# Four graph layers on one core: stores of the first block on ScalarE's queue, and the last layer's aggregation with the adjacency tiles stationary

## The chip, the cores and the metric

The kernel runs on one core of a Trainium2 chip. The metric is the time of one execution on the device in microseconds (us). The core has five engines that run side by side and wait for one another by semaphores: TensorE (PE, matmuls), VectorE (DVE), ScalarE (ACT), GpSimd (POOL) and SyncE (SP, which here only issues transfers). Transfers (DMAs) are carried out by 16 DMA engines; an engine that issues one goes on at once, but an engine takes its instructions strictly in order, so one that waits ahead of an issue holds up everything behind it.

## The reference

The input is x (3327 nodes x 256 features, fp32) and adj (3327 x 3327, int32, about 1% ones, symmetric, with ones on the diagonal). Each of four layers adds a graph layer to x:

```
h = relu(layernorm(x));  x = x + layer(h, adj)
layer 0: 8-head attention (GAT): softmax over neighbours of leaky(el_i + er_j)
layer 1: attention by cosine similarity, masked by adj
layer 2: 8-head attention whose hard maximum is kept, masked by adj
layer 3: deg = sum_j mask_ij
         agg = (mask @ h) / max(deg, 1)
         out = relu([h @ W_self + b_self, agg @ W_nb + b_nb] @ W_comb + b_comb)
```

## The kernel before

Nodes are cut into NT = 26 tiles of P = 128 (NP = 3328), features into KC = 2 blocks of 128. k.X holds x in SBUF. Where fp16 isn't precise enough a number is kept as a high and a low fp16 half, and a product takes three matmuls for each feature block (`hi_lo_products`: high x high, high x low, low x high; six in all).

**startup** (lines 286 to 689) reads adj, transposes it with TensorE and stores it as fp8 in k.adjT, and between these projects h for layer 0. Its order is written out by hand in `startup_order`, and each engine walks the same list: `adj a` (transposes of one tile of 128 rows, in two halves of 13 blocks, L426; VectorE evacuates half 0, L661, ScalarE half 1, L537), `turn g` (normalise and transpose four tiles), `project t`, `left g` (the left attention terms of 512 nodes, to elT), `scale`, and 16 `factor` items (two exponentials x 8 heads). For a factor VectorE or GpSimd multiplies (F, ring of NF = 3), ScalarE copies to fp16 (L566, into X1, ring of NX = 3), VectorE subtracts for the low half (L656, semaphore s_xl), and the result is stored to xv_dram. SP walks the list too: at `adj i` it loads tile i + 2 into one of two slots once tile i has been transposed (L356, semaphore s_atr), at `left` it stores elT to el_dram (L375) once it is evacuated, at `factor` it stores X1 to xv_dram (L379):

```
elif kind == "factor":
    f, h = FACTORS[i]
    sp.wait_ge(s_xl, i + 1)
    sp.dma_start(xv_dram[f, h], X1[:, i % NX].rearrange("p t d -> p (t d)")).then_inc(s_out[i % NX], 16)
```

The tail of the list is: scale, adj 15, factors 0 and 1, adj 16, factor 2, adj 17, factors 3 and 4, adj 18, and so on to factor 14, adj 25, factor 15. Before `scale` goes on, all left terms must have landed (s_elo). The next stage, gat_sums, begins when all stores have landed.

**The last layer** (layer3) has two blocks. `normalise` computes statistics, h (H, fp32), its transpose hT as high and low halves (ScalarE L201, VectorE L169), and then `h_nat`, here Hn: h in natural layout as high halves (ScalarE L216) and low halves (VectorE L174), three pieces each. `mean_weights` runs inside it by hooks: it multiplies W_self and W_nb with their halves of W_comb (m, high L1766 and low L1722), makes the bias (L1751, L1725), and turns the inverse degrees round and stores them to ideg_dram. `mean_aggregate` is the second block. A chunk is CT = 2 tiles (256 nodes), NC = 13 of them. For each chunk `sums` makes the transposed aggregate: for each feature block 26 x 2 matmuls with Hn stationary and 256 columns of adjacency moving (104 in all, L1830). VectorE multiplies by the inverse degree (L1874), ScalarE takes the high half (L1860), VectorE the low half (L1877), and `linear` adds, for each tile, 6 matmuls of hT with m's own half (L1840) and 6 of the aggregate with the neighbour half (L1843). `linear` of a chunk comes behind the next chunk's `sums`. VectorE adds the bias (L1882), applies relu and adds to X (L1886). SP loads adjacency chunks from adjT_dram into two slots (L1794) and stores finished chunks.

Of the kernel before, what the change touches and what calls it, by code (L numbers as in the profile page):

```python
# [23 lines left out]
U8 = mybir.dt.uint8  # L24
# [63 lines left out]
def normalise(k, tag, hT, weights, h_nat=None, also=None):  # L88
# [8 lines left out]
    pieces = ((0, 9), (9, 18), (18, NT))  # L97
    COUNTED = 8
    with ExitStack() as c:
# [23 lines left out]
        def _(dve):  # L123
# [54 lines left out]
        def _(act):  # L178
# [34 lines left out]
            if h_nat is not None:  # L213
# [77 lines left out]
def startup(k, x_dram, adj_dram, w_lin, attn_w, el_dram, xv_dram, HC):  # L291
# [12 lines left out]
    NF, NX = 3, 3  # L304
# [9 lines left out]
    with ExitStack() as c:  # L314
# [33 lines left out]
        def _(sp):  # L348
# [19 lines left out]
            for kind, i in order:  # L368
                if kind == "adj" and i + 2 < NT:
                    load(i + 2)  # L370
                elif kind == "left":
                    c0, cn = CHUNKS[i]
                    at = items.index((kind, i))
                    sp.wait_ge(s_free[at % 2], at // 2 + 1)
                    sp.dma_start(el_dram[:, c0:c0 + cn], elT[:, i % 2, 0:cn]).then_inc(s_elo[i % 2], 16)  # L375
                elif kind == "factor":
                    f, h = FACTORS[i]
                    sp.wait_ge(s_xl, i + 1)
                    sp.dma_start(xv_dram[f, h], X1[:, i % NX].rearrange("p t d -> p (t d)")).then_inc(s_out[i % NX], 16)  # L379
# [111 lines left out]
        def _(act):  # L491
# [41 lines left out]

            for kind, i in order:
# [13 lines left out]
                elif kind == "turn":  # L548
                    relu(i + 1)
                    high(i)  # L550
                elif kind in ("project", "left"):
                    evacuate(kind, i)
                elif kind == "scale":
                    act.wait_ge(s_fac, 1)
# [5 lines left out]
                else:  # L560
# [5 lines left out]
                    nc.scalar.activation(X1[:, i % NX, :, 0:G1], F[:, i % NF], ACT.Copy).then_inc(s_xh, 1)  # L566

# [385 lines left out]


def over_chunks(eng, chunk):

    with eng.Fori(0, NC // 2) as i:
        chunk(2 * i, 0, False)
        chunk(2 * i + 1, 1, False)
    chunk(NC - 1, 0, True)  # L960
# [717 lines left out]
def mean_weights(k, c, ap, m, bias, ideg_dram):  # L1678
# [3 lines left out]
    s_in, s_tr, s_cp, s_bb, s_mm, s_hi, s_deg, s_rT, s_out, s_b = (  # L1682
        k.sem(f"s_w3_{n}") for n in ("in", "tr", "cp", "bb", "mm", "hi", "deg", "rT", "out", "b"))
# [7 lines left out]
    dT = k.sb(c, "w3_degT", [NT, P], F32)  # L1691
    pt = k.ps(c, "w3_pt", [P, 2, CH])
    pm = k.ps(c, "w3_pm", [P, 2, CH])
    pd, pb = pm[:, 1, :], pt[:, 0, :]
# [3 lines left out]
    def on_sync(sp):  # L1698
# [28 lines left out]
    def tensor_first(pe):  # L1727
        pe.wait_ge(s_deg, 2)
        nc.tensor.transpose(pd[0:NT, 0:P], dg[:, 1, :], k.ident[:]).then_inc(s_tr, 1)
# [7 lines left out]
        for s in range(2):  # L1737
            pe.wait_ge(s_cp, s + 1)
            if s == 1:
                pe.wait_ge(s_rT, 1)  # L1740
# [13 lines left out]
    def scalar_first(act):  # L1754
        act.wait_ge(s_tr, 1)
        nc.scalar.activation(dT[:], pd[0:NT, 0:P], ACT.Copy).then_inc(s_rT, 1)

    def scalar_mid(act):
        for s in range(2):
            act.wait_ge(s_tr, s + 2)  # L1760
            nc.scalar.activation(wt[:, s].rearrange("p k n -> p (k n)"), pt[:, s, :], ACT.Copy).then_inc(s_cp, 1)

    def scalar_last(act):
        for s in range(2):
# [4 lines left out]
            "scalar_first": scalar_first, "scalar_mid": scalar_mid, "scalar_last": scalar_last,  # L1769
# [3 lines left out]
def mean_aggregate(k, hT, Hn, m, bias, ideg_dram, adjT_dram, out_dram):  # L1773

    nc = k.nc
    s_agg, s_T, s_hi, s_lo, s_mm, s_t, s_x, s_ideg, s_st = (
        k.sem(f"s_m3_{n}") for n in ("agg", "T", "hi", "lo", "mm", "t", "x", "ideg", "st"))
    s_in = [k.sem(f"s_m3_in{i}") for i in range(2)]
    prods = hi_lo_products(KC)
    with ExitStack() as c:  # L1780
        ad = k.sb(c, "m3_ad", [P, 2, CT, NT, P], FP8)
        idr = k.sb(c, "m3_ideg", [P, NP], F32)
        T = k.sb(c, "m3_T", [P, 2, KC, CW], F32)
        aT = k.sb(c, "m3_aT", [P, 2, 2, KC, CW], F16)
        R = k.sb(c, "m3_R", [P, 2, CT, D], F32)
        pa = k.ps(c, "m3_pa", [P, 2, KC, CH])
        po = k.ps(c, "m3_po", [P, 2, CT, D])
# [3 lines left out]
        def _(sp):  # L1791
            def load(c, q):
                sp.wait_ge(s_agg, c + 1)
                sp.dma_start(ad[:, q].rearrange("p t j i -> p t (j i)").bitcast(U8),  # L1794
                             adjT_dram[bass.ds(c * CT, CT)].rearrange("t p n -> p t n").bitcast(U8)).then_inc(s_in[q], 16)

            def store(c):
                sp.wait_ge(s_x, c + 1)
                sp.dma_start(out_dram[bass.ds(c * CW, CW), :].rearrange("(t p) d -> p t d", p=P),
# [148 lines left out]
```

## Time and profile before

| | us |
|---|---|
| median of three runs | 2383.29 (2383.27 to 2383.88) |
| the profiled execution | 2383.7 |
| its span | 2381.7 |
| PE busy | 2105.3 (88%) |
| DVE busy | 1960.3 (82%) |
| ACT busy | 1779.1 (75%) |
| POOL busy | 732.4 (31%) |
| `startup` | 0 to about 188 |
| last layer | about 2145 to 2381.7 |

The span runs from the first to the last instruction or transfer that the profiler saw. Busy shares are averages over stages with different limits; the rows below are from the two stages that the change touches. Matmuls are pipelined: a matmul's duration in a row is longer than the distance at which they follow each other.

### The profile page before, as it was taken

What the parts mean: (1) busy time and instruction counts of PE and PEld (TensorE: products, weight loads), DVE (VectorE), ACT (ScalarE), POOL (GpSimd) and SP (SyncE); (2) the same over time, 40 slices, a digit from 0 to 9 for tenths busy, and PEclk for the clock granted to TensorE, in tenths of its full rate; (3) what the DMA queues carried; (4) which work ended last, traced back from release to release, by engine and by line L of the source; (5) the groups of instructions that cost most, each with busy time, mean ns of one, the idle gap of its engine ahead of it and who ended that gap; (6) DMA issues with size and microseconds to landing.
All of it is one profiled execution on the core that took longest, in us unless ns stands there. A gap on an engine that the chain in (4) does not pass through costs nothing. (4 is left out here: it accounts for less than half of the span.)

```text
span 2381.7 us, 62641 instructions
## 1 busy us (share of the span) xinstructions
PE 2105.3 (88%) x25316; PEld 1713.9 (72%) x25316; DVE 1960.3 (82%) x4332; ACT 1779.1 (75%) x2232; POOL 732.4 (31%) x698
## 2 busy tenths in 40 slices
PE   4747999999967999999979699999999999885999
PEld 3547999999954888888865366666666666554888
DVE  5575999999985888888878699999999999985122
ACT  4546999999975877777755499999999999994000
POOL 0020000000000000000003588888888888870000
PEclk9858999999988999999989799999999999996999
DMA  9787211212101111011006411111111111102222
GB/s 319 261 325 302 88 66 62 92 58 91 59 6 47 47 43 43 22 43 43 22 14 143 153 53 52 63 66 66 66 66 66 66 66 65 37 2 78 71 78 66
DMA packets 78475, 201.09 MB, mean 84 GB/s; under 512 B 26897, under 2 KB 44491, under 8 KB 74745
## 3 DMA queue, kind: packets, MB, share of 16 engines
q1 hardware_dynamic: 77432, 197.27, 24.5%
q8 instruction: 191, 3.13, 0.5%
q14 instruction: 84, 0.69, 0.1%
q10 hardware_dynamic: 768, 0.00, 0.0%
HBM read 161.87 MB, written 26.86 MB: 79 GB/s over the span
## 5 line engine op out<-in xcount | busy, mean ns | idle before, releaser
L1638 DVE CUSTOM_DVE_ANT_0 h_S<-h_ps,h_off 128x832 f32<-128x832 f32 x832 | 800.4, 1020 | 14.0 <-POOL h_off L1477 11.0
L1535 PE MATMUL h_ps<-KS,h_QS 98*128 98x416 f16 x1664 | 442.1, 348 | 79.8 <-DVE h_mx L1638 45.3
L1595 ACT ACTIVATE h_H<-h_S,h_nmx 128x2048 fp8e4<-128x2048 f32 x208 | 416.8, 2004 | 81.0 <-DVE h_nmx L1644 81.0
L834 ACT ACTIVATE b_CA<-b_el,HC 128x1152 fp8e4<-128x1152 f32 (+1 forms) x384 | 435.5, 1218 | 3.0 <-DMA b_el<-el_dram 3.0
L931 PE MATMUL b_pb<-b_x,b_B 128*128 128x132 f16 x5408 | 414.2, 221 | 3.9 <-DVE b_B L896 3.4
L931 PEld LDWEIGHTS b_pb<-b_x,b_B 128*128 128x128 fp8e4 x5408 | 340.3, 96 | 6.6 <-DVE b_B L896 6.2
L1483 POOL TENSOR_SCALAR h_gap<-h_S,h_nmx 128x1280 f32<-128x1280 f32 x208 | 277.8, 1336 | 89.2 <-DVE h_nmx L1644 79.6
L912 PE MATMUL b_pz<-b_x,adjT 128*128 128x134 f16 x2704 | 257.1, 222 | 15.9 <-DMA b_x<-xv_dram 15.9
L1488 POOL TENSOR_SCALAR h_H<-h_gap 128x1280 uint8<-128x1280 f32 x208 | 260.8, 1254 | 17.2
L1566 PEld LDWEIGHTS h_po<-Vhl,h_HT 128*128 128x128 fp8e4 x5408 | 214.6, 98 | 65.1 <-ACT h_HT L1602 0.7
L1245 PE MATMUL c_pd<-c_mv,WnT 128*128 128x256 f16 x2028 | 250.8, 275 | 11.0 <-DMA c_ad<-adjT_dram 11.0
L1535 PEld LDWEIGHTS h_ps<-KS,h_QS 98*128 98x128 f16 x1664 | 95.9, 97 | 198.3 <-DVE h_mx L1638 120.4
L1566 PE MATMUL h_po<-Vhl,h_HT 128*128 128x64 f16 x5408 | 225.7, 193 | 0.6 <-ACT h_HT L1604 0.6
L1245 PEld LDWEIGHTS c_pd<-c_mv,WnT 128*128 128x128 f16 x2028 | 199.8, 99 | 36.0 <-DMA c_ad<-adjT_dram 11.3
L1602 ACT ACTIVATE h_HT<-h_pT 128x1024 uint16<-128x1024 uint16 x208 | 209.6, 1008 | 0.2 <-PE h_pT L1543 0.2
L912 PEld LDWEIGHTS b_pz<-b_x,adjT 128*128 128x128 fp8e4 x2704 | 183.6, 97 | 16.1 <-DMA b_x<-xv_dram 16.1
L849 DVE TENSOR_SCALAR b_CD<-b_el,HC 128x1152 uint8<-128x1152 f32 (+1 forms) x240 | 187.5, 781 | 7.4 <-DMA b_el<-el_dram 7.4
L1155 ACT ACTIVATE c_E<-c_T,c_shift 128x512 f32<-128x512 f32 x169 | 122.3, 724 | 94.1 <-DVE c_T L1182 91.7
L1261 PE MATMUL c_pa<-WHhi,c_EH 128*128 128x257 f16 x676 | 185.4, 274 | 0.0
L1263 PE MATMUL c_pa<-WHhi,c_EL 128*128 128x257 f16 x676 | 184.7, 273 | 0.0
L1262 PE MATMUL c_pa<-WHlo,c_EH 128*128 128x256 f16 x676 | 184.1, 272 | 0.0
L1121 POOL MEMSET c_shift<- 128x1 f32 x1 | 0.1, 99 | 593.6 <-POOLq L971 593.6
(208 smaller groups left out, 3496.7 us busy)
## 6 DMA issues: line engine op xcount, KB each, us to landing
h_rows<-in_adj_dram SPq DMA_DIRECT2D x25, 1663.5 KB, 7.3
b_x<-xv_dram SPq DMA_DIRECT2D x48, 435.5 KB, 5.3
s_rows<-in_adj_dram SPq DMA_DIRECT2D x25, 832.0 KB, 6.7
s_rows<-in_adj_dram SPq DMA_DIRECT2D x25, 831.5 KB, 7.9
adjT_dram<-adjT SPq DMA_DIRECT2D x1, 10816.0 KB, 38.0
c_ad<-adjT_dram SPq DMA_DIRECT2D x13, 832.0 KB, 6.1
m_ad<-adjT_dram SPq DMA_DIRECT2D x13, 832.0 KB, 4.5
b_el<-el_dram SPq DMA_DIRECT2D x16, 576.0 KB, 3.7
```

What stands on the lines that cost most here:

```text
L834: nc.scalar.activation(dst[:, 0:cols], elr[:, n % 2, 0:cols], ACT.Sigmoid, bias=HC[:, h, 1, jt:jt + 1], scale=STEP, saturate=False).then_i ...
L849: nc.vector.tensor_scalar(dst[:, 0:gn * P].bitcast(U8), elr[:, n % 2, 0:gn * P], HC[:, h, 0, jt:jt + 1], float(FP8_ONE), ALU.is_gt, ALU.mu ...
L912: last = nc.tensor.matmul(pz[:, z % 2, r * WZ:(r + 1) * WZ].rearrange("p (h d) -> p h d", h=2), k.adjT[:, g0 + 3 * b + r, jt, :], xb[:, m ...
L931: last = nc.tensor.matmul(pb[:, p, b, r * W:(r + 1) * W].rearrange("p (f d) -> p f d", f=2), B[:, u % RING_B, t * P:(t + 1) * P], xb[:, m ...
L1245: last = nc.tensor.matmul(pd[:, n % RD, j * CW:(j + 1) * CW], WnT[:, a, kc, jt * P:(jt + 1) * P], mv[:, c % 2, b, kc, :], start=(i == 0), ...
L1483: nc.gpsimd.tensor_scalar(gap[:], S[:, g % 2, CA:NP], nmx[:, g % 2:g % 2 + 1], -SHARPER, ALU.add, ALU.mult).then_inc(s_gap, 1)
L1488: nc.gpsimd.tensor_scalar(H[:, g % 2, CA:NP].bitcast(U8), gap[:], float(FP8_ONE), 0.0, ALU.min, ALU.max).then_inc(s_hB, 1)
L1535: last = nc.tensor.matmul(ps[:, ch % 2, b, 0:SB], QS[:, i % 2, h, :], KS[:, h, c0:c0 + SB], start=True, stop=True)
L1566: last = nc.tensor.matmul(po[:, i % 2, h * 2 * HD:(h + 1) * 2 * HD], wt[:, b, :, e], Vhl[:, b, e, h, :], start=(b == 0 and e == 0), stop=( ...
L1595: nc.scalar.activation(H[:, g % 2, 0:CA], S[:, g % 2, 0:CA], ACT.Exp, bias=nmx[:, g % 2:g % 2 + 1], scale=1.0, saturate=False).then_inc(s_ ...
L1602: nc.scalar.activation(HT[:, g % 2, 0:CA].bitcast(U16), pT[:, 0, :].bitcast(U16), ACT.Copy).then_inc(s_evA, 1)
L1638: nc.vector.tensor_tensor_reduce(out=two(S[:, g % 2, ch * SW:(ch + 1) * SW]), in0=ps[:, ch % 2, :, 0:SB], in1=two(off[:, i % 2, ch * SW:(c ...
```

## The change

First block: the stores of left terms and of factors are issued from ScalarE's queue. `left g` is stored in the turn two later, the last two at `scale`; factor n - 1 is stored after ScalarE's copy of factor n. X1 gets a fourth buffer.

Last layer: by associativity, (mask @ h) W is computed as mask @ (h W). `neighbour(t)` multiplies a tile of h with the neighbour half of m (six matmuls of 256 columns); ScalarE takes the high half of the result, scaled, VectorE the low half, side by side in Pn (512 columns). `sums(i)` takes, for each tile i of 128 nodes, 26 matmuls with an fp8 adjacency tile stationary and the 512 columns of Pn moving; `own(i)` the six matmuls with the own half of m. ScalarE scales the low half's sum by the inverse degree, VectorE adds the scaled high half's, bias, own part, relu and X. The 23 last `neighbour` groups are interleaved with the first tile's sums. Hn, the transposed inverse degrees and their way through DRAM go; the loops are written out.

```
-    NF, NX = 3, 3
+    NF, NX = 3, 4
...
-                elif kind == "left":
...
-                elif kind == "factor":
...
+            def store_left(g):
+                c0, cn = CHUNKS[g]
+                at = items.index(("left", g))
+                act.wait_ge(s_free[at % 2], at // 2 + 1)
+                act.dma_start(el_dram[:, c0:c0 + cn], elT[:, g % 2, 0:cn]).then_inc(s_elo[g % 2], 16)
+
+            def store_factor(n):
+                f, h = FACTORS[n]
+                act.wait_ge(s_xl, n + 1)
+                act.dma_start(xv_dram[f, h], X1[:, n % NX].rearrange("p t d -> p (t d)")).then_inc(s_out[n % NX], 16)
...
                 elif kind == "turn":
                     relu(i + 1)
+                    if i >= 2:
+                        store_left(i - 2)
                     high(i)
...
                 elif kind == "scale":
+                    store_left(NGROUPS - 2)
+                    store_left(NGROUPS - 1)
                     act.wait_ge(s_fac, 1)
...
                     nc.scalar.activation(X1[:, i % NX, :, 0:G1], F[:, i % NF], ACT.Copy).then_inc(s_xh, 1)
+                    if i >= 1:
+                        store_factor(i - 1)
+            store_factor(len(FACTORS) - 1)
...
-            if h_nat is not None:
-                for n, (t0, t1) in enumerate(pieces):
-                    dve.wait_ge(s_hi, nw + len(slots) + 1 + n)
-                    nc.vector.scalar_tensor_tensor(h_nat[:, 1, t0:t1], H[:, t0:t1], HSC, h_nat[:, 0, t0:t1], ALU.mult, ALU.subtract)
...
-                act.wait_ge(s_h, NT)
-                for t0, t1 in pieces:
-                    nc.scalar.activation(h_nat[:, 0, t0:t1], H[:, t0:t1], ACT.Copy, scale=HSC).then_inc(s_hi, 1)
...
-        sp.wait_ge(s_rT, 1)
-        sp.dma_start(ideg_dram.rearrange("(t p) -> t p", p=P), dT[:]).then_inc(s_out, 16)
-        sp.wait_ge(s_out, 16)
...
+        dve.wait_ge(s_deg, 2)
+        nc.vector.tensor_scalar(ideg[:], dg[:, 1, :], 1.0 / AGSC, None, ALU.mult)
...
+    RP, LEAD = 3, 3
...
         @block.sync
         def _(sp):
...
+            def load(c):
+                if c >= 2:
+                    sp.wait_ge(s_agg, CT * (c - 1))
...
+            store(NC - 2)
+            sp.wait_ge(s_x, NT - 1)
             sp.dma_start(out_dram[(NT - 2) * P:(NT - 1) * P, :], k.X[:, NT - 2, :]).then_inc(s_st, 16)
+            sp.wait_ge(s_x, NT)
             for p0, p1 in LAST_CUTS:
...
         @block.tensor
         def _(pe):
...
+            def neighbour(t):
+                if t >= RP:
+                    pe.wait_ge(s_pl, t - RP + 1)
+                for n, (kc, a, b) in enumerate(prods):
+                    last = nc.tensor.matmul(pp[:, t % RP, 0:D], hT[:, a, kc, t * P:(t + 1) * P], m[:, b, 1, kc, :],
+                                            start=(n == 0), stop=(n == len(prods) - 1))
+                last.then_inc(s_p, 1)
+
+            def sums(i):
+                c, q = i // CT, i % 2
+                pe.wait_ge(s_in[c % 2], 16 * (c // 2 + 1))
+                if i >= 2:
+                    pe.wait_ge(s_t, i - 1)
+                for jt in range(NT):
+                    if i == 0:
+                        if jt + LEAD < NT:
+                            neighbour(jt + LEAD)
+                        pe.wait_ge(s_pl, jt + 1)
+                    last = nc.tensor.matmul(pa[:, q, :], ad[:, c % 2, i % CT, jt, :], Pn[:, jt, :], start=(jt == 0), stop=(jt == NT - 1))
                 last.then_inc(s_agg, 1)
...
+            def own(i):
+                if i >= 2:
+                    pe.wait_ge(s_c, i - 1)
+                for n, (kc, a, b) in enumerate(prods):
+                    last = nc.tensor.matmul(po[:, i % 2, 0:D], hT[:, a, kc, i * P:(i + 1) * P], m[:, b, 0, kc, :],
+                                            start=(n == 0), stop=(n == len(prods) - 1))
+                last.then_inc(s_self, 1)
+
+            for t in range(LEAD):
+                neighbour(t)
+            for i in range(NT):
+                sums(i)
+                own(i)
...
+            for t in range(NT):
+                act.wait_ge(s_p, t + 1)
+                nc.scalar.activation(Pn[:, t, 0:D], pp[:, t % RP, 0:D], ACT.Copy, scale=AGSC / PSC).then_inc(s_ph, 1)
+            for i in range(NT):
+                act.wait_ge(s_agg, i + 1)
+                if i >= 2:
+                    act.wait_ge(s_t, i - 1)
+                nc.scalar.activation(A[:, i % 2, :], pa[:, i % 2, D:2 * D], ACT.Copy, scale=ideg[:, i:i + 1]).then_inc(s_a, 1)
...
+            for t in range(NT):
+                dve.wait_ge(s_ph, t + 1)
+                nc.vector.scalar_tensor_tensor(Pn[:, t, D:2 * D], pp[:, t % RP, 0:D], AGSC / PSC, Pn[:, t, 0:D],
+                                               ALU.mult, ALU.subtract).then_inc(s_pl, 1)
+            for i in range(NT):
+                q = i % 2
+                dve.wait_ge(s_a, i + 1)
+                nc.vector.scalar_tensor_tensor(B[:, q, :], pa[:, q, 0:D], ideg[:, i:i + 1], A[:, q, :], ALU.mult, ALU.add).then_inc(s_t, 1)
+                dve.wait_ge(s_self, i + 1)
+                nc.vector.scalar_tensor_tensor(R[:, q, 0, :], po[:, q, 0:D], 1.0 / PSC, bias[:], ALU.mult, ALU.add).then_inc(s_c, 1)
+                dve.wait_ge(s_t, i + 1)
+                dve.wait_ge(s_c, i + 1)
+                nc.vector.tensor_tensor(R[:, q, 1, :], R[:, q, 0, :], B[:, q, :], ALU.add).then_inc(s_s3, 1)
+                dve.wait_ge(s_s3, i + 1)
+                nc.vector.scalar_tensor_tensor(k.X[:, i, :], R[:, q, 1, :], 0.0, k.X[:, i, :], ALU.max, ALU.add).then_inc(s_x, 1)
```

## Rows read from the trace of the kernel before

**Rows 1.** The page's first line: the span.

```profile
span 2381.7 us, 62641 instructions
```

**Rows 2.** Windows in the first block: length, busy us of each engine, clock, DMA share, GB/s.

```profile
110.00:130.00 20.00, 6.32 (x55) 5.34 (x53) 16.04 (x21) 9.57 (x11) 5.29 (x4) 0.50 0.46 176
130.00:180.00 50.00, 24.01 (x200) 20.05 (x201) 33.22 (x25) 20.23 (x18) 11.09 (x6) 0.50 1.01 374
```

**Rows 3.** Timeline of SP's queue, 106 to 129 us: start, length of the stretch, instruction.

```profile
106.38 4.28 SPq L356 DMA_DIRECT2D s_rows<-in_adj_dram  x2
121.62 5.53 SPq L379 DMA_DIRECT2D xv_dram<-s_spare  x2
127.19 1.11 SPq L356 DMA_DIRECT2D s_rows<-in_adj_dram  x2
```

**Rows 4.** Timeline of TensorE: the transposes of adjacency tile 16.

```profile
118.71 2.93 PE L426 MATMUL s_tr<-ident,s_rows 128*128 128x128 bf16 x26 [8.41 <-DVE adjT L661]
```

**Rows 5.** Timeline of VectorE at the scaling; lines L379 and L496, durations in ns.

```profile
112.67 0.63 DVE L633 TENSOR_REDUCE s_rm<-s_GE 128x8 f32<-128x208 f32 x1 [7.36 <-DMA el_dram<-s_spare]
...
L379 SPq DMA_DIRECT2D xv_dram<-s_spare x16: 319/327/455, 121.6 to 184.6; - x16
...
DMA to landing us min/median/max: 2.7/6.0/10.0
...
L496 ACTq DMA_DIRECT2D s_attn<-in_L_gnn_attn_w_dram x16: 440/552/1207, 1.3 to 11.5; - x16
```

**Rows 6.** The chain of waits, last layer: start, us, piece.

```profile
2188.49 4.43 DMA m_ad<-adjT_dram
...
2220.99 11.35 PE m_pa L1830 x104
```

**Rows 7.** Timeline of the last layer, all engines, 2176 to 2218 us.

```profile
2176.19 1.95 DVE L169 SCALAR_TENSOR_TENSOR hT<-n_pt,hT 128x512 f16<-128x512 f32 x4 [0.66 <-ACT hT L201]
...
2176.64 2.38 PE L1751 MATMUL w_pt<-w_comb,w_bb 128*128 128x256 f32 x8
2177.16 5.92 ACT L216 ACTIVATE Hn<-n_h 128x2304 f16<-128x2304 f32 x3
2179.31 7.23 DVE L174 SCALAR_TENSOR_TENSOR Hn<-n_h,Hn 128x2304 f16<-128x2304 f32 x3 [1.17 <-ACT Hn L216]
2182.99 1.07 ACT L1766 ACTIVATE m_w<-w_pm 128x512 f16<-128x512 f32 x2
2186.45 1.28 DVE L1722 SCALAR_TENSOR_TENSOR m_w<-w_pm,m_w 128x512 f16<-128x512 f32 x2
2187.65 0.41 DVE L1725 TENSOR_TENSOR m_bias<-w_pt,w_bc 128x256 f32<-128x256 f32 x1
...
2193.06 25.31 PE L1830 MATMUL m_pa<-m_ad,Hn 128*128 128x256 fp8e4 x208 [14.05 <-DMA m_ad<-adjT_dram]
```

**Rows 8.** Second layer: line L1011 from 757 to 762 us; timeline of its first projection.

```profile
L1011 PE MATMUL p_pt<-hT,w_cos x25: 379/379/379, 756.7 to 761.9; 128*128 128x512 f16 x25
...
725.87 0.39 ACT L1019 ACTIVATE WHhi<-p_pw 128x256 f16<-128x256 f32 x1
...
726.65 0.42 DVE L1037 SCALAR_TENSOR_TENSOR WHlo<-p_pw,WHhi 128x256 f16<-128x256 f32 x1 [0.39 <-ACT p_junk L1022]
...
727.13 1.86 PEld L1001 LDWEIGHTS p_pw<-w_cos,hT 128*128 128x128 f16 x18 [0.27 <-DVE WHlo L1037]
```

**Rows 9.** Windows of TensorE alone: length, busy us, granted clock, DMA share, GB/s.

```profile
2180.00:2181.00 1.00, 0.00 (x0) 1.00 0.00 0
...
2193.00:2194.00 1.00, 0.94 (x5) 0.50 1.01 426
```

**Rows 10.** Timeline of the kernel's end.

```profile
2377.35 0.76 DVE L1882 SCALAR_TENSOR_TENSOR m_R<-m_po,m_bias 128x256 f32<-128x256 f32 x2 [1.02 <-PE m_po L1843]
...
2378.86 0.35 SPq L1813 DMA_DIRECT2D out_dram<-X  x1
2379.26 0.93 SPq L1815 DMA_DIRECT2D out_dram<-X  x2
```

More of the change, by code:

```diff
@@ L85, in dram, with normalise @@
         return self.nc.dram_tensor(name, shape, dt, kind="Internal").ap()
-def normalise(k, tag, hT, weights, h_nat=None, also=None):
+def normalise(k, tag, hT, weights, also=None):
     nc = k.nc
@@ L1669, in layer2, with mean_weights @@
         hard_attend(k, ap["adj"], KS, Vhl, be, q_dram)
-def mean_weights(k, c, ap, m, bias, ideg_dram):
+AGSC = 64.0
+def mean_weights(k, c, ap, m, bias, ideg):
     nc = k.nc
-    s_in, s_tr, s_cp, s_bb, s_mm, s_hi, s_deg, s_rT, s_out, s_b = (
-        k.sem(f"s_w3_{n}") for n in ("in", "tr", "cp", "bb", "mm", "hi", "deg", "rT", "out", "b"))
+    s_in, s_tr, s_cp, s_bb, s_mm, s_hi, s_deg, s_b = (
+        k.sem(f"s_w3_{n}") for n in ("in", "tr", "cp", "bb", "mm", "hi", "deg", "b"))
     raw = k.sb(c, "w3_raw", [P, 2, KC, D], F32)
@@ L1819, in _ @@
         def _(pe):
-            pe.sem_inc(s_agg, 2)
-            pe.sem_inc(s_mm, 2)
-            def sums(c, q):
-                pe.wait_ge(s_in[q], 8 * (c - q) + 16)
-                pe.wait_ge(s_T, c + 1)
-                k.settle(pe)
-                for kc in range(KC):
-                    for jt in range(NT):
-                        for a in range(2):
-                            last = nc.tensor.matmul(pa[:, q, kc, 0:CW].rearrange("p (t i) -> p t i", t=CT),
-                                                    Hn[:, a, jt, kc * P:(kc + 1) * P], ad[:, q, :, jt, :],
-                                                    start=(jt == 0 and a == 0), stop=(jt == NT - 1 and a == 1))
-                last.then_inc(s_agg, 1)
@@ L1835, in linear @@
-            def linear(c, q):
-                pe.wait_ge(s_lo, c + 3)
-                pe.wait_ge(s_t, c + 1)
-                for t in range(CT):
-                    for n, (kc, a, b) in enumerate(prods):
-                        nc.tensor.matmul(po[:, q, t, :], hT[:, a, kc, bass.ds((c * CT + t) * P, P)], m[:, b, 0, kc, :],
-                                         start=(n == 0), stop=False)
-                    for n, (kc, a, b) in enumerate(prods):
-                        last = nc.tensor.matmul(po[:, q, t, :], aT[:, q, a, kc, t * P:(t + 1) * P], m[:, b, 1, kc, :],
-                                                start=False, stop=(n == len(prods) - 1))
-                last.then_inc(s_mm, 1)
@@ L1847, in _ @@
-            sums(0, 0)
-            with pe.Fori(0, NC // 2) as i:
-                sums(2 * i + 1, 1)
-                linear(2 * i, 0)
-                sums(2 * i + 2, 0)
-                linear(2 * i + 1, 1)
-            linear(NC - 1, 0)
+            def neighbour(t):
[5 more added lines that the diff above has]
+                last.then_inc(s_p, 1)
@@ L1879, in result @@
-            def result(c, q):
-                dve.wait_ge(s_mm, c + 3)
-                for t in range(CT):
-                    last = nc.vector.scalar_tensor_tensor(R[:, q, t, :], po[:, q, t, :], 1.0 / PSC, bias[:], ALU.mult, ALU.add)
-                last.then_inc(s_t, 1)
-                dve.wait_ge(s_t, c + 3)
-                xs = k.X[:, bass.ds(c * CT, CT), :]
-                nc.vector.scalar_tensor_tensor(xs, R[:, q], 0.0, xs, ALU.max, ALU.add).then_inc(s_x, 1)
-            means(0, 0)
@@ L1910, in build @@
+        normalise(k, "n3", hT, [], also=lambda c1: mean_weights(k, c1, ap, m, bias, ideg))
+        mean_aggregate(k, hT, m, bias, ideg, adjT_dram, out_dram)
 def build(nc, ap, out_dram):
```

101 lines of the change are left out of this document (24 added, 77 removed).

## The prediction

> **What bounds the kernel now.** I read the page first: the span is 2381.7 us and the profiled execution took 2383.7 us, so 2.0 us lie outside the span [rows 1]; the median of the three timed runs is 2383.29 us, 0.4 us below the profiled execution. The change touches two stages and nothing between them: the first block (`startup`, about 0 to 188 us) and the last layer (about 2145 us to the end). A stage in between that starts earlier does the same work, so I take it as shifted whole, and sum the two stages by themselves.
>
> In the last layer the chain of waits tells it at once: one load of adjacency tiles, then TensorE without a gap to the end [rows 6]. So each us taken from TensorE's list there, and each us by which that list starts earlier, is a us of the kernel. VectorE and ScalarE are idle most of the time there, and their work counts only ahead of the first sum and behind the last matmul.
>
> In `startup` the windows show two regimes [rows 2]. From 130 to 180 us the DMA engines are busy all the time (share 1.01, 374 GB/s), so that no engine's order matters there. From 110 to 130 us their share is 0.46. The SP timeline says why [rows 3]: SP issued the load of adjacency tile 17 from 106.38 to 110.66 us, then stood at the store of factor 0, whose wait was over at 121.62 us, then at that of factor 1, and issued the load of tile 18 only at 127.19 us. That load needs just one thing, the transposes of tile 16, which ran from 118.71 to 121.64 us [rows 4]. It stood behind two stores.
>
> **First block, part by part.** (1) With the stores gone from SP, the first half of tile 18 is issued when the first half of the transposes is over: 118.71 + 2.93/2 = 120.2 us, not 127.19; the second half at about 121.7 us, not 127.8 (half of SP's 1.11 us behind 127.19). That is 7.0 and 6.1 us, and I take 6.5. What follows is bound by transfers and keeps its pace as long as the engines keep up; VectorE was busy 33.22 us and ScalarE 20.23 us of the 50 from 130 to 180 [rows 2], so they have room, and the stage moves forward by 6.5 us as a whole. The idle transfer time of the stretch, 0.54 x 20 = 10.8 us, is the ceiling of this term; nothing is the floor.
> (2) VectorE began the scaling 7.36 us late, waiting for the last store of the left terms [rows 5], which sat in SP's queue behind loads of adjacency. On a queue of its own it need not stand behind them. The stores of factors took 2.7 us to land at the least and 6.0 us in the median [rows 5]. So the gain is between nothing and the difference, some 3.3 us; I take 1.5, nearer to nothing because the transfer engines are shared by both queues.
> (3) ScalarE now issues 7 + 16 DMAs. On SP one took 0.33 us; the only DMAs that ScalarE issues in this trace took 0.55 us each, with many small pieces [rows 5]. Behind them on ScalarE are the evacuation of an adjacency tile, `high` or the next factor. 23 x 0.33 = 7.6 us (12.7 us at the other price) go into 50 + 60 us of stage, and of the 50 us whose row is shown ScalarE is idle for 30; five stand between `relu` and `high` in the turns, where TensorE has transposes of adjacency tiles to do meanwhile. I charge 0.5 us; without that cover it would be 5 x 0.33 = 1.7 us. The new wait on `s_xl` before the store of factor n-1 stands behind the copy of factor n, by when VectorE is at or past that subtraction. At the very end the stores of factors 14 and 15 now leave one behind the other, the former after copy 15 and no longer before it: at most one transfer more, 435 KB at 374 GB/s = 1.2 us; I charge 0.5. A fourth X1 buffer costs nothing.
> Sum for the block: 6.5 + 1.5 - 0.5 - 0.5 = 7 us earlier; ends 0 and 12.
>
> **Last layer, ahead of the sums.** After the last low half of hT (VectorE, 2176.19 + 1.95 = 2178.14 us) three ScalarE copies (5.92 us) and three VectorE subtractions (7.23 us) make `Hn`; only then come m's high and low halves (1.07 and 1.28 us) and the bias (0.41 us), to 2188.06 us [rows 7]. Without `Hn`, ScalarE makes m's high half from 2177.16 us on, VectorE its low half from 2178.14 to 2179.4 us, and the bias from there to 2179.8 us; TensorE's input to the bias is ready at 2176.64 + 2.38 = 2179.02 us [rows 7]. That is 8.3 us earlier. The inverse degrees' way through DRAM goes as well; no row has anyone waiting for it, and the one short VectorE step that replaces it stands before statistics whose cover is the wait for weights. I take zero for both; without the cover, 0.3 us.
> The first load took 4.43 us from 2188.49 us, and sums began at 2193.06 [rows 6]. The same delays put the load at 2180.2 and the first sum at 2184.8 us.
>
> **Last layer, TensorE.** Columns are the same: 1352 x 256 in the sums become 676 x 512, and the 2 x 156 x 256 of the weights stay. A chunk of 104 sums takes 11.35 us, 0.1091 us each [rows 6]; six weight matmuls of as many columns are 0.655 us. A 512-column matmul: 25 of them start between 756.7 and 761.9 us [rows 8], 5.2/24 = 0.217 us, with +-0.004 from rounding. It can't be less than 512 columns at 2.4 GHz, 0.213, and two of the 256-column matmuls are 0.218; I take 0.216 (the bounds are 144.0 and 147.5 us for 676). Sums: 1352 x 0.1091 = 147.5 becomes 676 x 0.216 = 146.0, 1.5 us less. The load of a stationary tile takes 1.86/18 = 0.10 us [rows 8] and now lies beside a matmul twice as long; that it is an adjacency tile has no row here beside 512 columns (rival C).
> Three of the 26 `neighbour` groups run while the first load is under way: 3 x 0.655 = 2.0 us less. The other 23 are in the first tile's sums. There a tile costs TensorE 0.655 + 0.216 = 0.87 us, ScalarE one 256-column copy (0.39 us) and VectorE one subtraction (0.42 us) [rows 8]. A group's result is wanted after two more groups and three sums, 2 x 0.655 + 3 x 0.216 = 1.96 us, and the two evacuations with a hand-over of 0.2 us need 1.0 us. So no stall; in the like projection of the second layer three groups stall for 0.27 us [rows 8], which would be 0.09 x 23 = 2.1 us here; ScalarE has two passes a group there and one here, so I take none.
> The clock: before, TensorE had stood for 14 us, the granted clock was 0.50, that is 1.2 GHz, when the sums began [rows 9], and the first 208 took 25.31 us [rows 7] and not 2 x 11.35 = 22.70; that is 2.6 us. In the us from 2180 it still was 1.00, that is 2.4 GHz [rows 9]. Now TensorE works in the gap, at full clock from 2180.1 to about 2182.1 us, and stands 2.7 us. Whether the clock is down again at 2184.8 us no row settles: 0 to 2.6 us to be had, I take 1.3.
>
> **The end.** Now, from the last sum: ScalarE's copy 0.39, then four VectorE steps of 256 columns; two of them in a row took 0.76 before [rows 10], and single ones 0.42 [rows 8]: 1.5 to 1.6, with hand-overs 2.2 us (an estimate), of which 0.655 us lie beside `own(25)`; 1.5 us remain. Before it was 1.5 as well, from 2377.33 (0.02 ahead of VectorE's step) to 2378.86 us [rows 10]. But three stores were issued there one after the other, 0.4 us apart; the one of tile 24 now goes ahead, 0.4 us less.
> Sum for the layer: 8.3 + 1.5 + 2.0 + 1.3 + 0.4 = 13.5 us; the bad end is 8.3 + 0 + 2.0 - 2.1 + 0 + 0.4 = 8.6 (no clock, stalled groups, the high price), the good end 8.3 + 3.5 + 2.0 + 2.6 + 0.4 = 16.8.
>
> **Total.** 2383.7 - 7 - 13.5 = 2363.2 us against the profiled execution; against the median of the runs, 0.4 us lower, 2362.8 us.
>
> **Rivals.** (A) The transfer engines are the bound over the whole first block. Loads that go out earlier then only share the engines with stores that also want them, the two queues interleave, and the end of the block stays. For it: share 1.01 from 130 to 180 us. Against it: 10.8 us of idle transfer time ahead of it, and a load that was ready to go 7 us before it was issued. It gives 2362.8 + 7 = 2369.8 us.
> A rule of the Trainium skill speaks for (A): in "DMA: Bandwidth & Descriptors", section "Issuing engines are not separate DMA queues", DMAs of all issuing engines run on the same 16 engines and interleave, and issuing from several saves only the time of issue. By it alone the block gains nothing. I hold that it speaks of bandwidth, and that what is removed here is a wait in SP's order; no run here shows it yet.
> (B) Both stages come out at their good ends: the block gets 10 to 12 us, because two queues also move the mixed traffic faster than 374 GB/s, and the clock stays up: 2362.8 - 4 - 2 = about 2356 us.
> (C) Slower than before: the loaded operand. Each 512-column sum has to wait for its own adjacency tile's load, 0.10 us, because a load of 8-bit data does not pass beside 512 16-bit columns. It would cost 676 x 0.10 = 68 us, 2431 us; it decides from 20.5/676 = 0.030 us for each sum on. Against it: 25 matmuls of 512 columns, each with a load of its own, keep 0.217 us [rows 8].
> (D) The last layer's preparation is bound by something else once `Hn` is gone (weights, the barrier, the first load, which may be slower than 4.43 us), and gives back half of the 8.3 us: 2362.8 + 4 = 2367 us.
>
> **How the numbers follow.** Forecast 0.55, (A) 0.20, (B) 0.12, (D) 0.09, (C) 0.02, the rest in nothing that I can name. Range 2355.5 to 2371.5 us: the forecast with its ends, (A), (D), and most of (B). A measurement of this kernel can tell about 0.2%, 4.8 us, from no change. Only (C) is slower; to be within 0.2% both stages would have to fail. Faster 0.95, same 0.03, slower 0.02.
>
> **What would show it.** In the changed trace: no SP store between the adjacency loads, tile 18 issued at about 119 to 121 us, transfers busy from about 122 us on, the last store of factors near 178 us rather than 184.6 [rows 5]; the scaling's wait shorter than 7.36 us. In the last layer: the gap between the last hT half and the first adjacency load 2 us rather than 10; the first sum 4.6 us behind its load; 26 x 0.216 = 5.6 us for a tile's sums, 6.3 us with its own part; the first tile near 20.7 us. I am wrong if the first block's end stays near 188 us, if a tile takes over 6.4 us, or if the first tile takes over 24 us.

## The result

| | before | changed |
|---|---|---|
| median of four runs, us | 2383.28 (2382.32 to 2383.88) | 2363.06 (2359.28 to 2365.72) |
| ratio | 1 | 0.9914 [0.9897, 0.9932] |
| the profiled execution | 2383.7 | 2360.47 |
| its span | 2381.7 | 2358.5 |
| first block: first loads of the next stage | 187.69 | 178.95 |
| last layer: its first transfer to the span's end | 236.04 | 223.02 |

The change is worth 20.2 us, where 20.5 were forecast (2362.8 us, range 2355.5 to 2371.5). One execution among the experiments below, the fifth of e1_first_block, took 5104.59 us and is left out of that run's figures; all others of one kernel lie within 0.3% of each other.

The page's first part for the changed kernel (busy us, share and instructions of each engine):

```profile
PE 2099.1 (89%) x24639; PEld 1644.9 (70%) x24639; DVE 1969.6 (84%) x4395; ACT 1786.9 (76%) x2267; POOL 730.2 (31%) x698
```

PE's busy time fell by only 6.2 us. The rest of the gain is idle time that went, and no busy share shows it.

**The first block.** The windows that answer to [rows 2] (length, busy us of each engine, clock, DMA share, GB/s):

```profile
110.00:130.00 20.00, 8.31 (x74) 7.63 (x75) 17.06 (x22) 9.68 (x11) 5.69 (x4) 0.57 0.72 262
130.00:170.00 40.00, 20.99 (x175) 17.32 (x173) 30.35 (x24) 20.35 (x18) 10.06 (x6) 0.50 1.00 411
```

The share from 110 to 130 us rose from 0.46 to 0.72. But look at the second line too, and at the same 40 us of before:

```profile
130.00:170.00 40.00, 18.80 (x156) 15.63 (x156) 26.74 (x20) 16.19 (x15) 9.43 (x5) 0.50 1.01 377
```

The DMA engines are busy all the time, as before, and yet move 411 GB/s, not 377 (374 over the 50 us of [rows 2]). SP's timeline answers to [rows 3], and VectorE's to [rows 5]:

```profile
93.78 68.03 SPq L347 DMA_DIRECT2D s_rows<-in_adj_dram  x24
178.95 0.33 SPq L783 DMA_DIRECT2D b_el<-el_dram  x1
```

```profile
111.57 0.63 DVE L633 TENSOR_REDUCE s_rm<-s_GE 128x8 f32<-128x208 f32 x1 [6.01 <-DMA el_dram<-s_spare]
```

Nothing but adjacency loads is left in SP's list (each load is half a tile). Tile 18's first half was issued at 119.3 us, in the middle of tile 16's transposes:

```profile
L347 SPq DMA_DIRECT2D s_rows<-in_adj_dram x3: 327/327/328, 119.3 to 124.1; - x3
...
117.72 2.93 PE L408 MATMUL s_tr<-ident,s_rows 128*128 128x128 bf16 x26 [9.64 <-DVE adjT L661]
```

**The last layer.** The timeline that answers to [rows 7], from the last low half of hT to the first group behind the load:

```profile
2165.99 1.95 DVE L168 SCALAR_TENSOR_TENSOR hT<-n_pt,hT 128x512 f16<-128x512 f32 x4 [0.66 <-ACT hT L196]
...
2166.97 1.08 ACT L1751 ACTIVATE m_w<-w_pm 128x512 f16<-128x512 f32 x2
2167.86 1.27 DVE L1715 SCALAR_TENSOR_TENSOR m_w<-w_pm,m_w 128x512 f16<-128x512 f32 x2
2169.06 0.41 DVE L1718 TENSOR_TENSOR m_bias<-w_pt,w_bc 128x256 f32<-128x256 f32 x1
2169.72 0.89 SPq L1782 DMA_DIRECT2D m_ad<-adjT_dram  x2
...
2169.77 2.13 PE L1809 MATMUL m_pp<-m_w,hT 128*128 128x256 f16 x18 [0.92 <-PEq L98]
...
2174.15 1.35 PE L1809 MATMUL m_pp<-m_w,hT 128*128 128x256 f16 x6 [2.25 <-DMA m_ad<-adjT_dram]
```

m's high half, its low half and the bias stand directly behind hT, as forecast, with no `Hn` between. The load goes out 1.8 us after hT's last low half (2165.99 + 1.95 = 2167.94 us), where it was 10.4 us before [rows 6, 7]. Three groups run beside the load, and TensorE then stands for 2.25 us. The chain of waits goes on from there (start, us, piece):

```profile
2169.72 4.38 DMA m_ad<-adjT_dram
...
2174.15 1.35 PE m_pp L1809 x6
2175.50 0.43 PE m_pa L1823
2175.92 1.28 PE m_pp L1809 x6
2177.20 0.43 PE m_pa L1823
2177.63 0.76 PE m_pp L1809 x6
2178.39 0.21 PE m_pa L1823
...
2195.84 0.39 ACT m_P L1844
2196.26 0.43 DVE m_P L1855
...
2196.74 0.39 PE m_pa L1823
...
2348.18 5.63 PE m_pa L1823 x26
```

Two things cost time. The first two groups and sums run at half pace, 1.28 + 0.43 and not 0.66 + 0.21 us. The granted clock was 0.55 on average from 2174 to 2177 us, near its 1.2 GHz level, and 1.00, that is 2.4 GHz, from 2178 us (windows: length, busy us of each engine, clock, DMA share, GB/s):

```profile
2174.00:2177.00 3.00, 2.85 (x14) 1.89 (x15) 0.42 (x1) 0.38 (x1) 0.00 (x0) 0.55 0.51 204
2178.00:2179.00 1.00, 1.00 (x11) 0.79 (x9) 0.24 (x2) 0.38 (x1) 0.00 (x0) 1.00 0.02 8
```

And there is one stall at the end of the groups: the last one has no more groups behind it to cover its evacuation (the copy and the subtraction that take its result out of PSUM). From there to the end a tile is 26 sums in 5.61 us and 6 own matmuls in 0.66 us.

### The profile page after: what moved, and what is told of

Its sections match the earlier page's. It is cut to its first block and busy times, and to the rows that moved or that the text cites. A ratio compares the mean times of both kernels' runs of the same rounds, so it can differ in the third digit from the quotient of the medians.

```text
span 2358.5 us, 61100 instructions
## 1 busy us (share of the span) xinstructions
PE 2099.1 (89%) x24639; PEld 1644.9 (70%) x24639; DVE 1969.6 (84%) x4395; ACT 1786.9 (76%) x2267; POOL 730.2 (31%) x698
```

## The experiments

Each kernel was timed in five rounds beside the kernel before on the same chip, in three batches (e1 to e4, e5 to e8, e9 to e12), each batch on another chip. The medians of before in the three batches were 2382.93, 2384.48 and 2383.17 us, with single runs from 2380.89 to 2386.92. So two kernels 2 us apart can't be told from each other by medians. Beside each ratio I therefore read three stretches of the profiled execution: up to the first loads of the next stage (the first block), from the last layer's first transfer to its first adjacency load (its preparation), and from there to the span's end (its sums).

### Each half alone

`e1_first_block` is the kernel before with the new `startup`; `e2_last_layer` the changed one with the old `startup`.

> The new first block alone, the last layer as before. Theory (the two parts are independent and add up): the first loads of the next stage go out near 179.0 us and not 187.7, and the time is 2383.3 - 9 to - 10 = about 2374 us. Rival (the parts interact through the phase of TensorE's clock): the first block's gain changes on its way through the kernel by more than 1 us, and times scatter over some 5 us, as those of the changed kernel do.

> The new last layer alone, the first block as before. Theory: the last layer takes 223 us and not 236, 13 us less, and the time is about 2370.3 us. Rival (most of the gain is the first block's): 2375 us or more. If this kernel's times scatter over some 5 us and those of the first block alone do not, the scatter is of the last layer.

Measured: the first block alone 2374.23 us, ratio 0.9961 [0.9948, 0.9974], 8.7 us. The last layer alone 2371.51 us, ratio 0.9952 [0.9939, 0.9965], 11.4 us. The sum, 20.1 us, is about the 20.2 of both together: the halves don't touch each other. The first loads of the next stage are at 180.41 us with the new block and at 187.66 with the old; the new last layer takes 224.2 us. The times of e1 spread over 3.9 us and those of e2 over 3.1 us, so the scatter belongs to neither half alone.

### Is it the queue or the order?

`e3_one_queue` is the kernel before, with all stores on SP; it takes each factor's store two items later in SP's list, with the fourth buffer:

```
-    NF, NX = 3, 3
+    NF, NX = 3, 4
...
                 elif kind == "factor":
-                    f, h = FACTORS[i]
-                    sp.wait_ge(s_xl, i + 1)
-                    sp.dma_start(xv_dram[f, h], ...)
+                    if i >= 2:
+                        store_factor(i - 2)
+            for n in range(len(FACTORS) - 2, len(FACTORS)):
+                store_factor(n)
```

> Kernel before, but all stores stay on SP's queue; SP stores factor n only after two more factor items, so that no adjacency load stands behind an unfinished factor, and X1 has four buffers. Theory A (the wait in SP's order was the whole cause): the same gain as with ScalarE's queue, less the 1.1 us of the left terms: first loads of the next stage near 180 us, time about 2375 us. Theory B (two queues also move the mixed traffic faster, 411 GB/s in place of 374): tile 18 is issued at 120 to 122 us as well, but the rate from 130 us on stays near 374 GB/s, first loads near 183 us, time about 2378.5 us.

Measured: 2373.73 us, ratio 0.9957 [0.9944, 0.997], first loads at 178.29 us: with one queue as much as with two (e1: 2374.23 and 180.41 us). Its windows and SP's timeline:

```profile
110.00:130.00 20.00, 7.44 (x66) 6.76 (x67) 16.20 (x21) 9.67 (x11) 4.74 (x4) 0.50 0.71 262
130.00:170.00 40.00, 21.08 (x191) 17.88 (x189) 32.78 (x25) 19.35 (x17) 10.94 (x6) 0.59 1.01 414
```

```profile
107.24 14.65 SPq L356 DMA_DIRECT2D s_rows<-in_adj_dram  x4
121.93 0.43 SPq L371 DMA_DIRECT2D xv_dram<-s_spare  x1
124.99 2.47 SPq L356 DMA_DIRECT2D s_rows<-in_adj_dram  x2
```

Four loads of half a tile go out ahead of the first store, where two did [rows 3]. And the traffic runs at 414 GB/s in one queue. So the part of (B) that says two queues move it faster is refuted. e3 and e1 have the fourth X1 buffer in common too, and no run has that buffer with the old order. But in the trace of before, hardly anything waits for a buffer; ScalarE's copies waited for factors' stores (us, times):

```profile
  ACT s_spare L566: 0.6, 1
```

So a fourth buffer alone had 0.6 us to give there. The rule quoted under (A), that issuing from several engines saves only the time of issue (the Trainium skill, "DMA: Bandwidth & Descriptors", section "Issuing engines are not separate DMA queues"), agrees with this pair: the medians of e3 and e1 are 0.5 us apart. That by it alone the block gains nothing, as I put it under (A), doesn't follow. It speaks of bandwidth, and what the stores took was a place in a list.

`e4_factors_only` puts the factors' stores on ScalarE and leaves those of the left terms on SP, as before.

> The new first block, but the left terms are still stored from SP's queue; the last layer as before. Theory: the stores of left terms from ScalarE's queue are worth the 1.1 us by which the scaling began earlier, so this takes 1 us longer than the first block alone, about 2375 us. Rival (the left stores on ScalarE cost as much as they bring, in the turns): same time as the first block alone within 0.3 us.

Measured: 2374.55 us, ratio 0.9963 [0.995, 0.9976]; the wait of the scaling is back at 7.10 us, and the first loads at 180.10 us are where e1 has them (180.41).

```profile
113.27 0.63 DVE L637 TENSOR_REDUCE s_rm<-s_GE 128x8 f32<-128x208 f32 x1 [7.10 <-DMA el_dram<-s_spare]
```

So the left terms' store on ScalarE brings nothing that shows at the block's end. The medians are 0.3 us apart, as the rival says. But executions with one and the same new block differ by 3.1 us there (below), so neither that nor the 1 us of the theory is settled.

### The copies taken out of the last layer's preparation

`e6_dead_copies` is the changed kernel with the `Hn` steps put back into `normalise`; nobody reads them, and nothing is left out.

```
-        normalise(k, "n3", hT, [], also=...
+        Hn = k.sb(c, "Hn", [P, 2, NT, D], F16)
+        normalise(k, "n3", hT, [], Hn, also=...
```

> Changed kernel, with the three ScalarE copies and three VectorE subtractions of Hn kept as dead work. Theory: the whole preparation term of the last layer comes back, 8.3 to 8.6 us: about 2371.5 us. Rival (something else, weights or the first load, would have set the start anyway): it costs less than 6 us.

Measured: 2367.76 us, ratio 0.9928 [0.9915, 0.9942]: slower than the changed kernel, by less than expected: 4.7 us between the medians, which is below the rival's 6 us. The traces say where it goes, and not for the rival's reason. The preparation is 42.6 us (2136.67 to 2179.30), as long as before. But from the load to the end it took 187.3 us and not 188.8:

```profile
2179.30 4.53 DMA m_ad<-adjT_dram
...
2183.88 0.83 PE m_pp L1818 x6
2184.71 0.21 PE m_pa L1832
```

```profile
2179.35 3.71 PE L1818 MATMUL m_pp<-m_w,hT 128*128 128x256 f16 x18 [9.17 <-PEq L99]
```

```profile
2180.00:2183.00 3.00, 3.00 (x16) 1.95 (x14) 0.85 (x2) 0.77 (x2) 0.00 (x0) 0.56 0.89 280
2184.00:2186.00 2.00, 2.00 (x18) 1.60 (x17) 0.42 (x1) 0.77 (x2) 0.00 (x0) 1.00 0.56 227
```

TensorE had stood 9.17 us, the clock was low when the three groups began, and they took 3.71 us and not 2.13. They lie under the load, so the low clock cost nothing there, and was over when the load landed. The 8.3 us is therefore right for the preparation (42.6 against 34.2 us), and 1.5 us of it is given back behind it by where the low clock falls. That leaves 6.9 us by the traces; the 2 us between this and the medians are no more than medians here can't tell.

### The gap beside the load

LEAD says how many groups go ahead of the first tile's sums. `e5_all_ahead` has all 26, `e10_seven_ahead` seven; `e12_load_first` keeps three but has TensorE wait for the load before the first.

```
-    RP, LEAD = 3, 3
+    RP, LEAD = 3, NT          (e5; in e10: 3, 7)
```

```
+            pe.wait_ge(s_in[0], 16)          (e12)
             for t in range(LEAD):
                 neighbour(t)
```

> Changed kernel, with all 26 neighbour groups ahead of the first tile's sums (LEAD = NT), so that TensorE works on while the first adjacency load is under way. Theory: TensorE's gap of 2.25 us before the load lands is filled, the clock does not fall in it (1.6 us), and the wait for the last low half (0.3 us) goes: 2 to 4 us faster than the changed kernel, about 2360 us. Rival (the clock falls by what TensorE did before, not by this gap): 2.3 us faster at most, with 3.4 us at the low level early in the groups.

> Changed kernel, with seven neighbour groups ahead of the wait for the load and not three (7 x 0.655 = 4.6 us, about the landing time). Theory (the gain of all groups ahead is the filled gap): within 0.7 us of all groups ahead, near 2357 us, and as little scatter. Rival (it is the end of the groups, or the interleaving with 512-column sums): near the changed kernel.

> Changed kernel, but TensorE waits for the first adjacency load ahead of the first neighbour group, so that nothing is hidden beneath it. Theory: three groups come back, 2.0 us, and TensorE stands 4.9 us more, so that the clock is at its low level for as long as before: 0 to 2 us more; together 2 to 4 us slower than the changed kernel, 2365 to 2367 us. Rival (the clock's phase decides more than the gap): less than 1 us slower, or over 5.

| | median, us | ratio | load to end |
|---|---|---|---|
| changed kernel | 2363.06 | 0.9914 [0.9897, 0.9932] | 188.78 |
| the same again (e9) | 2362.1 | 0.991 [0.9896, 0.9923] | 188.81 |
| e5, all ahead | 2356.72 | 0.9884 [0.9869, 0.9899] | 184.23 |
| e10, seven ahead | 2357.43 | 0.9892 [0.9877, 0.9907] | 184.20 |
| e12, load first | 2362.7 | 0.9915 [0.9901, 0.9928] | 191.09 |

```profile
2170.32 17.19 PE m_pp L1809 x156
2187.51 5.61 PE m_pa L1823 x26
```

That is the chain of e5: TensorE goes through without a gap, at full pace, and the chain has no load in it. In this stretch 4.5 us are gained, more than the 2 to 4 expected: the gap of 2.25, the 1.9 us of low clock behind it, and the stall of 0.3. The medians are 6.3 us apart; what is beyond 4.5 lies ahead of this stretch, where the two kernels are alike. Seven groups do as well as 26, as far as these runs tell, so what counts is that the gap is filled.

The median of e12 is no slower than the changed kernel's and 0.6 us slower than e9's, which meets the rival's "less than 1 us". The trace sides with the theory: from the load to the end it takes 2.3 us longer.

```profile
2167.91 4.41 DMA m_ad<-adjT_dram
2172.36 4.78 PE m_pp L1809 x24
```

Its first 24 group matmuls take 4.78 us; at 0.655 us for six they would be 2.62. The first block and the middle of that execution were shorter by 1.0 and 1.9 us than in the changed kernel's, and the preparation was 1.1 us longer, which together hides most of it. That scatter is not the edit's.

### One matmul of 512 columns, or two of 256

`e7_two_by_256` is the changed kernel with each sum in two matmuls over the same adjacency tile.

```
+                    for v in range(2):
-                    last = nc.tensor.matmul(pa[:, q, :], ad[...], Pn[:, jt, :], ...)
+                        last = nc.tensor.matmul(pa[:, q, v * D:(v + 1) * D], ad[...], Pn[:, jt, v * D:(v + 1) * D], ...)
```

> Changed kernel, with each 512-column sum as two matmuls of 256 columns on the same adjacency tile, 1352 in all as before. Theory: a tile's sums take 52 x 0.109 = 5.67 us and not 5.61, in all 1.6 us more, about 2364.7 us: the wide matmul is worth no more than its share of fixed cost. Rival (the width hides weight loads that would show at 256 columns with 8-bit tiles loaded): 0.01 us or more for each matmul, 10 us in all.

```profile
2342.70 5.68 PE m_pa L1824 x52
```

Measured: 2362.39 us, ratio 0.9914 [0.9899, 0.9929]. In the trace a tile's sums take 5.68 and not 5.61 us, 26 x 0.07 = 1.8 us, and from the load to the end it is 190.55 us against 188.78. The medians can't resolve that; the rival's 10 us they would have shown.

### A version that beats both, and two repeats

`e8_last_tile_last` is e5 with adjacency tile 25 behind factor 15 in `startup_order`, since after 170 us the block is no longer bound by transfers: the changed kernel's DMA share from 170 to 180 us is 0.30.

```
-        while a < NT and (a - (NT - rest)) * len(FACTORS) <= n * rest:
+        while a < NT - 1 and (a - (NT - rest)) * len(FACTORS) <= n * rest:
```

> As all groups ahead, and in the first block adjacency tile 25 comes behind factor 15 in the list, so that the last factor's copy, subtraction and store no longer wait for the last tile. Theory (the end of the first block is now set by the chain tile 25, evacuation, copy 15, low half 15, store): the next stage's first loads leave 3 to 5 us earlier, near 175 us, and the time is 3 to 5 us below all groups ahead. Rival (the transfers are the bound to the end): less than 1 us.

Measured: 2351.63 us (2351.18 to 2353.43), ratio 0.9865 [0.985, 0.988], the fastest of all and 5.1 us below e5. First loads are at 174.49 us, 4.4 us earlier than in e5; from the start of the scaling to them it is 64.3 us and not 66.8, and the other 1.9 us lie ahead of the scaling, where the two kernels are alike. So by the trace the edit itself is worth 2.5 us.

`e11_one_queue_best` is e8 with the one-queue order of e3, to see whether ScalarE's queue is needed at all.

> All groups ahead and tile 25 last, but in the first block all stores on SP's queue, those of factors two items later. Theory (only the order counts, not the queue): 2351.6 us as with ScalarE's queue, within 1 us. Rival (ScalarE's queue has a value of its own): 2 us or more slower.

Measured: 2357.55 us, ratio 0.9888 [0.9873, 0.9903], 6 us behind e8 (5.5 by the ratios). That was a miss. First loads are at 180.49 us; from the load to the end it is 184.27 us, as in e8 (184.26), so the loss is in the first block. From the start of the scaling to the first loads it is 67.5 us against 64.3, so 3.1 of the 6.0 us lie there; the other 2.9 lie ahead of the scaling, whose start moves between 109.9 and 113.8 us with one and the same new block. Who waits for the factors' stores to land (us, times), in e8 and then in e11:

```profile
L525 ACTq DMA_DIRECT2D xv_dram<-s_spare x16: 326/326/353, 120.8 to 171.3; - x16
...
who waited for it (us, times):
  ACT s_spare L563: 2.5, 3
```

```profile
L362 SPq DMA_DIRECT2D xv_dram<-s_spare x16: 319/326/636, 122.5 to 177.3; - x16
...
who waited for it (us, times):
  ACT s_spare L563: 18.8, 6
```

```profile
172.46 1.76 ACT L563 ACTIVATE s_spare<-s_spare 128x858 f16<-128x858 f32 x2 [2.99 <-DMA xv_dram<-s_spare]
```

A store issued two items late holds its X1 buffer longer, and ScalarE's copies wait 18.8 us in all for buffers; the copies of the last two factors start at 172.46 us, where e8 had copied its last by 168.7. In e3 the same wait stands in the trace (21.8 us in 8 waits), but there the last adjacency tile came ahead of the last factor, and the end was no later for it. That reading fits both, but no run gave e11 more buffers, so it is read and not tested. Nor is it the only difference: from 130 to 150 us e11's transfers moved 403 GB/s and e8's 422, both at a share of 1.02. As far as these two traces go, the two ways of taking stores out of the way of loads differ after all: ScalarE can store a factor one item behind and hold up no load.

`e9_changed_again` is the changed kernel once more.

> The changed kernel itself once more, beside its variants on one chip. Theory: median near 2363 us with times on both sides, 2359 to 2366 us, and the runs at the upper end show the lower mean clock (0.948 against 0.951 to 0.952 so far). Rival (the upper times of the first measurement were chance): all within 2 us around 2360.5.

Measured: 2362.1 us (2360.05 to 2364.44), ratio 0.991 [0.9896, 0.9923]; load to end 188.81 us, against 188.78 us. The times fall on both sides, as expected, but the lower mean clock of the slow ones didn't come back: it was 0.951 at 2362.1, 2363.78 and 2364.44 us alike, and 0.952 at the two fastest. The sums repeat to 0.1 us; what moves between executions lies ahead of them. The clock behind the gap moved a little too: TensorE stood for 2.29 us, ran the first group at full pace, 0.83 us in the timeline as in steady groups, and only then fell to half pace, for as long.

## Why the prediction was right, step by step

The forecast held, and the mechanism of each half was the right one: loads held up behind stores, and a list of preparing steps ahead of the sums. That the total is right to 0.3 us is luck, since two errors cancel. The block gave more than the 7 us forecast (8.7), the layer less than 13.5 (13.0 in the pair of traces, 11.4 between the medians of e2 and before). By the profiled executions:

| step | predicted, us | measured, us |
|---|---|---|
| first block, all | 7 (0 to 12) | 8.7 |
| the middle, unchanged | 0 | 1.4 |
| `Hn` gone | 8.3 | 8.6 |
| 512 columns | 1.5 | 1.6 |
| three groups under the load | 2.0 | 2.0 |
| clock | 1.3 (0 to 2.6) | about 0.7 |
| stall of groups | 0 (down to -2.1) | -0.3 |
| the end | 0.4 | 0.3 |
| last layer, all | 13.5 | 13.0 |

**First block, step (1), the load of tile 18.** The place was right: behind stores whose work had nothing to do with it. It went out at 119.3 us, 7.9 us earlier, 1.0 of which is that tile 16's transposes began earlier; predicted were 7.0. What followed did not keep its pace, though. The prediction took 374 GB/s with a share of 1.01 as the ceiling of the stretch, "so that no engine's order matters there", and it was none. In windows of 2 us of before, two between 130 and 170 us fall below 300 GB/s at a share of 1.0 or more (at 142 and 154 us), and none of the changed kernel's falls below 408 GB/s from 126 to 168 us, though the one at 122 us moved 296 at a share of 1.22 (before, then changed):

```profile
142.00:144.00 2.00, 0.00 (x0) 0.00 (x0) 1.76 (x2) 2.00 (x2) 0.00 (x0) 0.50 1.06 286
```

```profile
142.00:144.00 2.00, 1.13 (x11) 0.86 (x9) 2.00 (x3) 0.83 (x1) 0.36 (x1) 0.50 1.01 420
```

So the term was too small, and the good end of (B) was reached in its rate but by another cause. Over the eight profiled executions with the changed block the first loads stand between 177.28 and 180.41 us (median 178.9), against 187.66 and 187.69 with the old: 7.3 to 10.4 us. Part of that is scatter ahead of the scaling. From the start of the scaling to the first loads it is 66.4 to 68.1 us with the new block and 75.0 and 75.7 with the old, so 7.0 to 9.2 us are gained there, where 6.5 less 1.0 for ScalarE's cost were forecast.
**Step (2), the left terms.** Predicted 1.5 us. The wait fell from 7.36 to 6.01 us, 1.35 us, but e4 without it ends the block at the same time as e1. The term is nothing that these runs can measure.
**Step (3), ScalarE's cost.** No harm shows: an issue took 0.33 us as on SP, and e3, which issues nothing on ScalarE, gained as much. (1) was some 2 us too small, and (2) covered it in part.

**The last layer.** The preparation's 8.3 us was exact to 0.3 us in the pair, 42.83 and 34.24 us. Over all executions preparations with `Hn` are 42.6 to 43.6 us and those without 34.2 to 35.5 us, so the pair is not a lucky one. That it comes back in full with the dead copies of e6 refutes (D) as it was put, although e6 shows a small cousin of it: 1.5 us come back by the clock. The 512-column sum took 5.61/26 = 0.2158 us with an 8-bit adjacency tile stationary, where 0.216 was taken; (C), which needed 0.030 us more for each, is out. A tile with its own part is 6.27 us.
The clock was the loose step. I said that no row settles whether it is down when the load lands. It was: the first groups behind the load took 1.28 us, and about 1.9 us were lost, against 2.6 before. Together with the stall the first tile took 23.0 us, not 20.7. The 1.96 us of cover against 1.0 us of need held in the steady groups; the stall came only where no groups are left behind the last.
At the end ScalarE's copy took 0.47 us and VectorE's first step 0.48, where I had 0.39 and about 0.4:

```profile
2353.83 0.47 ACT L1849 ACTIVATE m_A<-m_pa,m_ideg 128x256 f32<-128x256 f32 x1 [5.79 <-PE m_pa L1823]
2354.34 0.48 DVE L1860 SCALAR_TENSOR_TENSOR m_B<-m_pa,m_ideg,m_A 128x256 f32<-128x256 f32 x1 [4.11 <-ACT m_A L1849]
```

Both read their factor from an SBUF column here, where those in the rows of before had a constant. For VectorE the next step of the same tile is the like one, fp32 to fp32 with a constant, and takes 0.41 us; ScalarE's constant row in this kernel writes fp16, so there the column is not alone in being different. From the last sum to X's last step it was 2.33 us, with 2.2 forecast.

**What is not the change's.** The profiled execution of before had the longest middle of all fourteen: from the next stage's first loads to the last layer's first transfer it took 1957.97 us, in the others 1954.6 to 1957.7. So 1.4 of the 23.2 us between the two profiled executions are no effect of the change. The medians, 20.2 us apart, are the better measure, and the forecast from them is right by 0.3 us, more closely than its terms deserve.

**Open.** Why loads and stores moved at 377 and 379 GB/s from 130 to 170 us in the two executions with the old order and at 401 to 420 in the twelve with the new, at shares of 0.97 to 1.02: e3 shows that it isn't the number of queues, and no run changed the order alone, with the buffers and the time of the first load held fixed.

## What to carry to other kernels

In a queue that is served in order, look for an issue whose own condition is long met and which stands behind one that waits. Moving the waiting one to another engine or further down the same list cured it equally well in e1 and e3. A store that is later holds its buffer longer: with four buffers, ScalarE's copies waited 18.8 us for them in e11 and 2.5 us in e8. Where a product may be taken in either order, count the steps that only prepare an operand and stand on the path: they were 8.6 of 13 us here, while the matmuls themselves saved 1.6. And when TensorE gets work ahead of a load, give it enough to reach the load's landing: a gap of 2.25 us cost 4.5.

## What the runs showed of the hardware

- A DMA share of 1.0 says that packets are under way, not that the engines move what they can: 374, 379, 411, 414, 417 and 420 GB/s all stood beside shares of 1.00 to 1.02, each over 40 us or more.
- After TensorE stood for 2.25 us with full clock before, the granted clock was near 1.2 GHz when it went on, and the next groups ran at half pace. In e9, after 2.29 us, it fell from 1.00 only about 1 us after TensorE had gone on. In e5, e8, e10 and e11, where there is no gap, it stayed at 2.4 GHz. In e6 the low clock fell on work under a load and cost nothing. So where the low clock falls can be worth more than how much of it there is.
- An fp8 stationary tile beside 512 fp16 columns costs nothing beyond the columns: 0.2158 us a matmul over 26 in a row, 0.2133 being 512 columns at 2.4 GHz. Two of 256 columns over the same tile took 0.2185 us.
- Engines that evacuate 128 x 256 fp32 from PSUM took 0.38 us (ScalarE, to fp16) and 0.41 to 0.42 us (VectorE) with a constant as factor, and 0.47 and 0.48 us (to fp32) with a column as factor.
